# Cross attention's mask product contracted over 128 partitions instead of 8

## What is computed

```
xn   = layernorm(context) ; ln = layernorm(latents)
q    = rmsnorm_per_head(ln @ W_q)              # 2 heads of 64
k, v = split(concat(xn, ln) @ W_kv) ; k = rmsnorm_per_head(k)
s    = q @ k.T * 64**-0.5
s    = where(mask of valid keys, s, very negative)
out  = softmax(s) @ v @ W_out + b_out
```

## Time and profile before

| what | value |
|---|---|
| median of 3 runs | 670.51 us (663.33 to 674.94) |
| the profiled execution | 668.31 us |
| its span, first to last instruction | 666.4 us, mean granted TensorE clock 0.88 |
| TensorE busy: matmuls, weight loads | 566.7 us (85%), 437.1 us (66%) |
| VectorE, ScalarE, GpSimd busy | 373.7 us (56%), 233.6 us (35%), 262.7 us (39%) |
| DMA | 22.20 MB, mean 33 GB/s |
| L1212 matmuls (scores proper) | 208 instructions, 58.3 us, 367 ns each |
| L1201 matmuls (keys) | 208 instructions, 36.9 us, 328 ns each |
| L1227 matmuls (weighted sum) | 208 instructions, 34.3 us, 327 ns each |

### The profile page before, as it was taken

The page is one execution under the profiler, slowest core; times in us unless marked ns, Lnnn a source line. Parts: engine busy times, 40 slices in busy tenths (PEclk is TensorE's granted clock), DMA queues, the critical chain, the costliest instruction groups (busy, mean ns, idle before and its releaser), DMA issues. The chain is left out here.

```text
span 666.4 us, 13787 instructions
## 1 busy us (share of the span) xinstructions
PE 566.7 (85%) x5334; PEld 437.1 (66%) x5334; DVE 373.7 (56%) x957; ACT 233.6 (35%) x544; POOL 262.7 (39%) x350
## 2 busy tenths in 40 slices
PE   0889998999999893988757999899898966959997
PEld 0666865866696673777645777677686754536676
DVE  4576676665457764365643677655645653634342
ACT  1366356445443651332213433222222321421210
POOL 3562372255125511035543576937537412400000
PEclk9999999997599997899985999575767976978999
DMA  5501011010620002101110001011000000000000
GB/s 154 222 1 30 17 50 29 18 48 1 190 94 2 1 2 60 73 2 53 52 50 1 1 1 50 0 50 49 3 1 1 1 0 2 1 1 1 0 2 17
DMA packets 8488, 22.20 MB, mean 33 GB/s; under 512 B 1248, under 2 KB 4152, under 8 KB 8160
## 3 DMA queue, kind: packets, MB, share of 16 engines
q1 hardware_dynamic: 8416, 21.23, 9.7%
HBM read 20.97 MB, written 0.26 MB: 32 GB/s over the span
## 5 line engine op out<-in xcount | busy, mean ns | idle before, releaser
L823 POOL TENSOR_TENSOR rstd<-ss,par 128x1 f32<-128x1 f32 x52 | 28.5, 549 | 107.8 <-ACT sq L675 107.6
L1212 PE MATMUL sc<-rope,pr 128*128 128x128 f32 x208 | 58.3, 367 | 0.0
L1426 POOL TENSOR_TENSOR rk<-rk,par 128x8 f32<-128x8 f32 (+1 forms) x32 | 45.7, 1427 | 2.7
L1212 PEld LDWEIGHTS sc<-rope,pr 128*128 128x128 f32 x208 | 35.9, 217 | 8.2
L1349 DVE TENSOR_TENSOR sd<-sc,rk 128x512 f32<-128x512 f32 (+1 forms) x32 | 18.9, 591 | 37.8 <-PE sc L1212 16.4
L1284 ACT ACTIVATE pr<-pt 128x512 f32<-128x512 f32 (+1 forms) x32 | 16.5, 515 | 61.8 <-PE pt L1201 61.7
L1201 PE MATMUL pt<-xw,pr 128*128 128x128 f32 x208 | 36.9, 328 | 0.0
L1227 PE MATMUL pt<-xh,sd 128*128 128x130 f32 x208 | 34.3, 327 | 1.5 <-ACT sd L1288 1.5
L1201 PEld LDWEIGHTS pt<-xw,pr 128*128 128x128 f32 x208 | 33.1, 237 | 2.2 <-issue 1.1
L692 ACT ACTIVATE pr<-sd 128x1024 f32<-128x1024 f32 (+1 forms) x36 | 31.2, 866 | 9.5 <-DVE sd L770 7.2
L1227 PEld LDWEIGHTS pt<-xh,sd 128*128 128x128 f32 x208 | 32.5, 241 | 2.6 <-issue 2.5
(11 more groups left out here) (255 smaller groups left out, 1394.3 us busy)
## 6 DMA issues: line engine op xcount, KB each, us to landing
cx<-ctx_in SPq DMA_DIRECT2D x8, 768.0 KB
we<-we_in SPq DMA_DIRECT2D x8, 514.0 KB, 8.4
wc<-wc_in SPq DMA_DIRECT2D x4, 768.5 KB, 5.6
wa<-wa_in SPq DMA_DIRECT2D x5, 387.0 KB, 3.0
wb<-wb_in SPq DMA_DIRECT2D x4, 256.5 KB, 3.6
uvT<-uvT_in SPq DMA_DIRECT2D x1, 1024.0 KB, 4.7
uv<-uv_in SPq DMA_DIRECT2D x1, 1024.0 KB, 6.9
xw<-xw_in SPq DMA_DIRECT2D x1, 323.0 KB
```

The source lines that it names most:

```text
L823: nc.gpsimd.tensor_tensor(rstd[:, t:t + 1], ss[:, t:t + 1], par[:, 1:2], ALU.pow).then_inc(s[piece], 1)
L1212: last = nc.tensor.matmul(part, xnT[n % 3][:, P * j:P * j + P], qp[:, i, :, :].rearrange("p h q -> p (h q)"), start=False, stop=True, skip ...
L1426: nc.gpsimd.tensor_tensor(rk[:, n, 0:2 * w], rk[:, n, 0:2 * w], par[:, 1:2].to_broadcast([P, 2 * w]), ALU.pow).then_inc(xm[piece], 1)
```

## The change

Three buffers get 128 partitions instead of 8, and the two arrays behind them are padded with rows on the host: the mask with False and the selecting table with zeros. The mask product then contracts over 128 partitions; rows 8 to 127 of `notm` are ones and those of `sel` zeros, so that they add nothing. No instruction is added, removed or moved: on PE, ACT and POOL the lists of instructions are the same line by line; on DVE L1465 is now 128 x 1664 instead of 8 x 1664, and on SP the loads of L1120 and L1121 are 128 x 1664 bytes and 128 x 1024 bf16 numbers instead of 8 x 1664 and 8 x 1024.

```diff
@@ program(): buffers of the cross attention
-        mraw = xsb("mraw", [B, CT * P], U8)
-        notm = xsb("notm", [B, CT * P], BF16)
-        sel = xsb("sel", [B, B, P], BF16)
+        mraw = xsb("mraw", [P, CT * P], U8)
+        notm = xsb("notm", [P, CT * P], BF16)
+        sel = xsb("sel", [P, B, P], BF16)
@@ constants()
-    sel = np.zeros((B, B, P), np.float32)
+    sel = np.zeros((P, B, P), np.float32)
     sel[np.arange(B), np.arange(B)] = NEG
@@ layout()
-    mask = np.zeros((B, CT * P), bool)
-    mask[:, :S2] = i["mask_BxS2_bk0"][:, key]
+    mask = np.zeros((P, CT * P), bool)
+    mask[:B, :S2] = i["mask_BxS2_bk0"][:, key]
```

## The result

| | before | after |
|---|---|---|
| median | 668.82 us (4 runs, 663.33 to 674.94) | 644.90 us (4 runs, 637.03 to 651.06) |
| ratio, with its 95% interval | | 0.957 (0.944 to 0.970) |
| span of the profiled execution, granted clock | 666.4 us, 0.880 | 635.2 us, 0.922 |
| TensorE busy, matmuls | 566.7 us | 519.5 us |
| cross attention, start of the first `c_power` to start of the last `x_added` (DVE, L1399) | 293.6 to 554.5, 260.9 us | 286.1 to 523.4, 237.3 us |

What follows compares the result with a forecast made beforehand. TensorE was taken to bound the first stretch, then a ring of TensorE, VectorE and GpSimd. Savings of 8.3, 10.4 to 22.2 and 3.8 us gave 22.5 to 34.3, middle 28.4: median 642 us, range 636 to 648.

Steps and rivals of the forecast that it cites:

- The lost time is one of shape and goes: Score tiles: 0.29 us lost switching between 128- and 8-partition products disappears with equal shapes; 642 us, chance 0.66.
- The new price of a tile: Score tile on TensorE: falls to its pure stream, 0.28 us at full clock from 0.57, 0.54 at half from 0.94.
- First stretch: Start of cross attention, 43 mask products, TensorE the bound: two thirds of 12.5 us reach the end, 8.3 us.
- Three rings: Half-clock rounds of TensorE, VectorE and GpSimd waiting on each other: save 10.4 us at the old clock, 22.2 at GpSimd's floor.
- The floor that I worked out: Ring: GpSimd's 17.8 us plus VectorE's 4.3 us, so no turn under 22.1 us however fast TensorE is.
- The end: Last sequence of cross attention: 13 tiles wait for nothing but TensorE and save 0.29 us each, 3.8 us.
- The clock: TensorE's half clock from 414.4 us on: expected to rise earlier, since without lost time the work streams more densely.
- the middle of both: Total saving taken midway between 22.5 us (clock as now) and 34.3 us (rings at GpSimd's floor): 28.4 us.
- What comes free: L1465 on 128 partitions stays at 1.01 us, and the larger loads, 2 us once, are hidden: no cost.
- The sum: Whole kernel: 28.4 us saved, from first stretch, three rings and end, giving a median of 642 us.
- the slower rival: First stretch of cross attention: the clock falls there too, making the kernel 6.6 us slower, 677 us; chance 0.04.

Runs made afterwards that it cites:

- e2: Kernel after with the mask product contracted over 64 partitions instead of 128; 660.29 us in one run, kernel before beside it 666.20.
- e3: Kernel after with the mask product contracted over 96 partitions instead of 128; 653.47 us in one run, kernel before beside it 666.20.
- e4: Kernel before with both mask tables in fp32 instead of bf16, still 8 partitions; 715.93 us in one run, kernel before beside it 666.20.
- e5: Kernel after with both mask tables in fp32 instead of bf16, 128 partitions; 650.08 us in one run, kernel before beside it 665.04.
- e7: Kernel after with each group's mask products first, then its scores (part of the mask is lost); 646.62 us, ratio not settled.
- e11: Kernel after once more, unchanged; 647.26 us against 670.09 for the kernel before, ratio 0.959.
- e8: Kernel after with the mask product left out, so the mask doesn't reach the scores; 644.17 us, ratio to before 0.959.
- e9: Kernel after with VectorE's last group of moments moved ahead of the last c_scaled and top by one due time; 640.05 us, ratio not settled.
- e1: Kernel after with the mask product cut back to 8 partitions, padded buffers and larger loads kept; 664.41 us, ratio to before 1.002.
- e12: Repeat of e9: kernel after with the last moments moved ahead of top; 639.09 us, ratio to before 0.953.

## Why the prediction was right, point by point

*The lost time is one of shape and goes.* Right, as e2, e3, e4 and e5 show: in bf16 the loss comes with 8 or 64 rows and not with 96 or 128, in fp32 with 8 and not with 128. The rule of the Trainium skill that I set beside the rows (TensorEngine Tiling, Key Properties: changing the tiling mode drains TensorE) agrees with these runs: 0.57 us a tile with 8 or 64 rows, 0.33 with 96 or 128. The one on row groups (TensorE: Matmul & The Clock Gate, Part 3, what overlaps), by which nothing would have been won, does not: the mask's weights now go to the same row groups as the scores' and yet the products start 0.06 us apart.

*The new price of a tile.* I took 0.28 us and 0.54 at the half clock, bounded from above by 0.385 and 0.64. It is 0.33 and 0.64. This term was mis-sized by 0.05 and 0.10 us; the bf16 matmul itself was right (0.058, e7), the missing piece is the alternation. TensorE's saving by tile is thus 0.24 and 0.30 us instead of 0.29 and 0.395.

*First stretch, 8.3 us.* This is the term that missed most. From the first `c_power` to the fourth it was 95.6 us and is 94.8, 0.8 us less; with the first round (25.9 to 23.1 us) 3.6 us in all (1.5 us in e11). I called TensorE the bound there because it was occupied 50.77 of 51.70 us. But occupied is not working: 43 tiles held 0.24 us each that the shape cost and that went with it, and the records of matmuls cover it. The piece up to the fourth `c_power` takes 94.8 us in e8 too, with no mask product, so something else paces it; the waits point at the chain of `c_sums`, `c_rnorm` and `c_scaled`, which no run changed by itself. GpSimd's waits for the sums of squares between the first scores and the fourth `c_power`, before and after:

```profile
POOL rk L1424 <- DVE kss L1344: 13.9, 4, 6.3
```
```profile
POOL rk L1424 <- DVE kss L1344: 13.1, 4, 6.3
```

They hardly moved, and TensorE has new waits there instead (1.8 us for `top`, L1358, and 1.0 for `c_scaled`, L1349).

*Three rings, 10.4 to 22.2 us.* Right in place and size: 29.5, 28.0 and 29.8 us became 23.4, 23.1 and 22.6, so 18.2 us. The floor that I worked out, 22.1 us, lies 0.5 to 1.3 us under what they reach, and e8 shows that there is a floor for TensorE: with still less work on it they don't move. What lies between is VectorE: in the first of the three the last `c_scaled` starts at 423.21, 1.4 us behind GpSimd's last `c_rnorm` (421.83), with other instructions ahead of it in VectorE's queue. It is the floor of this order of work alone: with the moments moved, the same three rounds take 19.8, 20.6 and 19.2 us (e9).

*The end, 3.8 us.* From the last `c_power` to the last `x_added`: 52.2, now 50.2, so 2.0 us.

*The clock.* It came back earlier, as forecast: 71.7 us at half between 414 and 510 us became 30.7 us. That took the rings to their floor and not to the 26 us that I had worked out for them at the old clock. I had taken the middle of both; the rings used all of it. How much of this is the clock can be read in e1, which has the 8-row product of before: one of its rounds had the clock at half for only 3.4 us and took 23.10 us, as long as a round after. Its neighbour, with 17.1 us at half, took 28.45.

```profile
409.42:437.87 28.45, 23.99 (x121) 19.12 (x121) 17.57 (x53) 7.85 (x17) 17.31 (x21) 0.70 0.09 30
437.87:460.97 23.10, 20.76 (x135) 16.49 (x135) 16.34 (x51) 7.84 (x17) 17.49 (x20) 0.93 0.11 37
```

So in that round, near the full clock, even the slow products fitted under the ring's floor. What the change gained in the three rings it gained where the clock stood at half, and by shortening that time.

*What comes free.* L1465 took 1.018 us on 128 partitions after 1.006 on 8, and VectorE still idled 1.63 us behind it; e1 (ratio 1.002) shows the loads hidden.

*The sum.* 28.4 us forecast, 23.6 us in the stage: 3.6 + 18.2 + 2.0 (the parts round to 0.2 us more), against 8.3 + 16.3 + 3.8. The rings gave more than the middle, and the first stretch and the end together less than half of their terms. The median forecast, 642 us, stands 2.9 us under the measured one. That is nearer than the working deserved: the rings, 1.9 us over their term, made good part of the 6.5 us that the other two fell short, and the middle between two clocks was a choice and not a mechanism. (In the sum of the slower rival the saving elsewhere is 20.2 us and not 20.1, which changes nothing.)

## What to carry to other kernels

A small product between full ones is worth trying with as many rows as its neighbours have, by zero rows if need be, or in groups: 8 rows against 128 cost 0.24 us for each tile here, and the padding was free. A share of busy time near 100% does not make an engine the bound where its records cover standstill; measure starts against a clean stream of the same shape, and then ask what the chain through the other engines allows. Before padding anything, look at where a small late instruction is queued: one due time gave as much as the whole change (27.9 and 23.6 us of the stage), and left the change little to give.

## What was not expected

- 64 rows cost as much as 8 (0.57 us a tile): there is no half price for half of the array, and the step lies between 64 and 96 rows.
- The kernel's total holds several microseconds that no edit touches. The stages outside the cross attention took 397.7 to 417.5 us over fourteen profiled executions of nearly the same instructions; with e2, the shortest, the clock was at half for 42.2 us of them, with e12, the longest, for 97.1. In a kernel like this the length of the stage settles what the total can't.
- Once the ring is at its floor its rounds repeat to 0.1 us whatever TensorE has to do: the last three take 23.4, 23.1 and 22.6 us in after, in e7, in e8 without the mask product, and in e11. Only the first varies (24.8 us in e11, 23.1 in the others).
